# Cross attention and FP4 FFN on one core: x and h turned by DMA transposes instead of TensorE

## What is computed

```python
x = x + xattn(layernorm(x), ctx, ctx, Wt, Wp, Wg, Wz, gamma, beta)   # three 256x256 products, group statistics
x = x + ffn(layernorm(x))
# ffn: q() is blockwise FP4 (16 numbers a block), scale and grid, along the last dimension
gate = q(x) @ q(w_gate).T ; y = q(x) @ q(w_up).T                     # 1408 columns each
h = silu(gate) * y ; out = q(h) @ q(w_down).T                        # back to 512
```

## Time and profile before

| | us |
|---|---|
| median of 3 runs | 1983.17 (1981.67 to 1985.04) |
| the profiled execution, its own time | 1983.16 |
| its span, first to last instruction | 1981.2 |
| TensorE busy / VectorE busy in it | 1844.4 / 1610.4 |
| an odd tile and the even one behind it, mid loop | 28.36 + 27.57 |

### The profile page before, as it was taken

One profiled execution on the slowest core, in us unless ns is written; L12 is line 12 of the kernel. 1 busy time (PEld: TensorE's weight loads), 2 busy tenths in 40 slices (PEclk: granted clock), 3 DMA queues, 4 the chain that ended last, 5 costly groups with the idle time before them and its releaser, 6 DMA issues.

```text
span 1981.2 us, 32391 instructions
## 1 busy us (share of the span) xinstructions
PE 1844.4 (93%) x11022; PEld 1208.4 (61%) x11022; DVE 1610.4 (81%) x2885; ACT 620.4 (31%) x981; POOL 737.0 (37%) x1065
## 2 busy tenths in 40 slices
PE   2528899999999999999999999999999999999997
PEld 1427566666666666666666666666666666666664
DVE  5575888888888888888888888888888888888775
ACT  2324332333333332333233333333333333323221
POOL 4647443333333343433333343333333433333310
PEclk9769999999999999999999999999999999999999
DMA  5100010001000000000000000000010000100000
GB/s 183 51 0 22 17 33 16 32 32 32 16 32 32 32 25 23 32 32 32 16 32 32 32 21 26 32 32 32 16 32 32 32 16 32 32 32 27 11 11 17
DMA packets 32022, 60.11 MB, mean 30 GB/s; under 512 B 3072, under 2 KB 4352, under 8 KB 32000
## 3 DMA queue, kind: packets, MB, share of 16 engines
q1 hardware_dynamic: 32000, 59.81, 8.9%
HBM read 43.03 MB, written 16.78 MB: 30 GB/s over the span
## 4 chain that ended last, share of the span: by engine, by line
PE 41%; issue 20%; POOL 15%; DVE 12%; DMA 6%; ACT 4%; SPq 1%; DVEq 1%; POOLq 0%; ACTq 0%
PE pairs L449 19%; PE obank L461 12%; DMA c_in<-in_ctx 5%; POOL c_lo L1123 5%; PE pairs L413 5%; PE ubank L413 2%; ACT early L694 2%; DVE hT_parts L753 2%; ACT c_hi L610 2%; POOL q_lo L1129 1%; DVE ln_st L809 1%; DVE x L805 1%; DVE xT_lo L753 1%; POOL att L1151 1%; DVE early L906 1%
## 5 line engine op out<-in xcount | busy, mean ns | idle before, releaser
L461 PE MATMUL obank<-w_parts,hT_parts 128*128 128x512 f16 x2112 | 467.1, 380 | 0.0
L461 PEld LDWEIGHTS obank<-w_parts,hT_parts 128*128 128x128 f16 x2112 | 207.0, 98 | 235.4 <-issue 1.1
L449 PE MATMUL pairs<-w_gate_hi,xT_hi 128*128 128x352 f16 x1024 | 321.0, 313 | 7.8 <-DVE xT_lo L753 7.1
L449 PE MATMUL pairs<-w_gate_hi,xT_lo 128*128 128x352 f16 x1024 | 320.8, 313 | 0.0
L449 PE MATMUL pairs<-w_up_lo,xT_hi 128*128 128x352 f16 x1024 | 320.7, 313 | 0.0
L449 PE MATMUL pairs<-w_up_hi,xT_lo 128*128 128x352 f16 x1024 | 320.7, 313 | 0.0
L449 PE MATMUL pairs<-w_gate_lo,xT_hi 128*128 128x352 f16 x1024 | 320.7, 313 | 0.0
L449 PE MATMUL pairs<-w_up_hi,xT_hi 128*128 128x352 f16 x1024 | 320.5, 313 | 0.0
L897 DVE SCALAR_TENSOR_TENSOR h<-pairs,w_unit,early 128x352 f32<-128x352 f32 x256 | 149.5, 584 | 199.7 <-ACT early L694 195.6
L694 ACT ACTIVATE early<-pairs,w_unit 128x352 f32<-128x352 f32 x256 | 140.1, 547 | 366.3 <-PE pairs L449 366.3
L1123 POOL TENSOR_TENSOR c_lo<-c_in,c_hi 128x512 fp32r<-128x512 f32 x64 | 98.2, 1554 | 179.8 <-ACT c_hi L610 172.9
(11 more groups left out here) (172 smaller groups left out, 3615.7 us busy)
## 6 DMA issues: line engine op xcount, KB each, us to landing
x_in<-in_x SPq DMA_DIRECT2D x32, 512.0 KB, 3.4
c_in<-in_ctx SPq DMA_DIRECT2D x32, 512.0 KB, 3.5
out<-early SPq DMA_DIRECT2D x64, 256.0 KB, 2.1
raw<-in_L_ffn_w_down SPq DMA_DIRECT2D x2, 1408.0 KB, 8.8
raw<-in_L_ffn_w_gate SPq DMA_DIRECT2D x2, 1280.0 KB, 8.3
w_parts<-in_L_ffn_w_up SPq DMA_DIRECT2D x2, 1280.0 KB, 9.2
raw<-in_L_ffn_w_gate SPq DMA_DIRECT2D x2, 128.0 KB, 8.4
early<-in_L_xattn_Wt SPq DMA_DIRECT2D x1, 256.0 KB, 9.8
```

The costliest lines, as they stand in the source:

```text
L449: mm = pe.matmul(pairs[:, pair, n, 0:GW], xT[s][part][:, k, :], w1[n][wpart][:, k, c * GW:(c + 1) * GW], start=(k == 0 and part == 0 and w ...
L461: mm = pe.matmul(obank[:, :], hT[part][:, k, :], w2[wpart][:, k, :], start=(k == 0 and part == 0 and wpart == 0), stop=(k == KH - 1 and pa ...
```

## The change

x and h are no longer turned on TensorE. ScalarE casts hq (two pieces of 704 columns) and xq from SBUF to f16, VectorE subtracts, both also from SBUF, and both halves lie side by side in raw's second third (hq_parts, xq_parts). SyncE's queue then issues one DMA transpose for h (128 x 2816 numbers) and one for x (128 x 1024) in each tile, behind the load of the tile and ahead of the store. TensorE waits once for each. On ScalarE h's casts stand ahead of ctx_hi and the first Silu, x's ahead of the fourth Silu, and affine behind it. On VectorE h's subtractions stand behind h_finish, ahead of the first gated product; x's ahead of the residual. Blank and unchanged lines are left out of this diff, and some of its waits and of the start's lines:

```diff
--- before.py
+++ after.py
@@ -141,7 +141,8 @@
-        xT = [[sb(f"xT{s}_{part}", [P, KD, P], F16) for part in ("hi", "lo")] for s in range(2)]
+        xT_parts = [sb(f"xT_parts{s}", [P, 2, KD, P], F16) for s in range(2)]
+        xT = [[xT_parts[s][:, part] for part in range(2)] for s in range(2)]
@@ -157,6 +158,10 @@
+        hq_parts = raw[:, 1, 0:H].bitcast(F16).rearrange("p (a k) -> p a k", a=2)
+        xq_parts = raw[:, 1, H:H + D].bitcast(F16).rearrange("p (a k) -> p a k", a=2)
+        HPIECES = ((0, H // 2), (H // 2, H))
@@ -351,6 +356,20 @@
+            def turn_x(t, s):
+                made = t + 1 if isinstance(t, int) else sp.to_reg(t + 1)
+                wait_apart(sp, minus_made, x_lo_done, made)
+                sp.dma_start_transpose(xT_parts[s][:].rearrange("p a k n -> p (a k) n"),
+                                       xq_parts.rearrange("p a k -> p (a k)")).then_inc(x_turned, 16)
+            def turn_h(j):
+                made = 2 * j + 2 if isinstance(j, int) else sp.to_reg(2 * j + 2)
+                wait_apart(sp, minus_made, h_lo_done, made)
+                sp.dma_start_transpose(hT_parts[:].rearrange("p a k n -> p (a k) n"),
+                                       hq_parts.rearrange("p a k -> p (a k)")).then_inc(h_turned, 16)
@@ -372,9 +391,11 @@
+            turn_x(0, 0)
+                more = not isinstance(i, int) or i + 1 < NB
@@ -382,6 +403,10 @@
+                        turn_h(j - 1)
+                    if more or s == 0:
+                        turn_x(j + 1, 1 - s)
+                    if not isinstance(j, int) or j > 0:
@@ -389,6 +414,7 @@
+            turn_h(NT - 1)
@@ -425,21 +451,6 @@
-            def turn_x(t, bank):
-                pe.wait_ge(xq_ready, t + 1)
-                for k in range(KD):
-                    mm = pe.transpose(bank[:, k * P:(k + 1) * P], xq[:, k * P:(k + 1) * P], ident[:, :])
-                mm.then_inc(x_turned, 1)
-            def turn_h(j, r):
-                pe.wait_ge(hq_ready, 3 * j + r + 1)
-                k0, nk = SETS[r]
-                for k in range(nk):
-                    mm = pe.transpose(tbank[:, (r + 1) % 2, k, :], hq[:, (k0 + k) * P:(k0 + k + 1) * P], ident[:, :])
-                mm.then_inc(h_turned, 1)
@@ -454,12 +465,11 @@
-                for r, (k0, nk) in enumerate(SETS):
-                    pe.wait_ge(h_lo_done, 3 * j + r + 1)
-                    for k in range(k0, k0 + nk):
-                        for part, wpart in PARTS:
-                            mm = pe.matmul(obank[:, :], hT[part][:, k, :], w2[wpart][:, k, :],
-                                           start=(k == 0 and part == 0 and wpart == 0), stop=(k == KH - 1 and part == 1))
+                pe.wait_ge(h_turned, 16 * j + 16)
+                for k in range(KH):
+                    for part, wpart in PARTS:
+                        mm = pe.matmul(obank[:, :], hT[part][:, k, :], w2[wpart][:, k, :],
+                                       start=(k == 0 and part == 0 and wpart == 0), stop=(k == KH - 1 and part == 1))
...
@@ -538,7 +546,7 @@
-                    pe.wait_ge(x_lo_done, j + 1)
+                    pe.wait_ge(x_turned, 16 * j + 16)
@@ -551,32 +559,20 @@
-                        if c > 0 and not first:
-                            if c != 2:
-                                at_least(pe, h_lo_done, 3 * (j - 1) + (c - 2 if c == 3 else 0))
-                            turn_h(j - 1, c - 1)
+                        if isinstance(j, int) and j == 1:
+                            pe.wait_ge(w_lo_done, len(weight_sets))
-                    if more or s == 0:
-                        if first:
-                            pe.wait_ge(w_lo_done, len(weight_sets))
-                        at_least(pe, h_lo_done, 3 * (j - 1) + 2)
-                        turn_x(j + 1, tbank[:, 0].rearrange("p k n -> p (k n)"))
-            for r in range(3):
-                pe.wait_ge(h_lo_done, 3 * (NT - 1) + max(r - 1, 0))
-                turn_h(NT - 1, r)
@@ -603,6 +599,17 @@
+            def x_hi(t):
+                act.wait_ge(xq_ready, t + 1)
+                at_least(act, x_turned, 16 * t)
+                nc.scalar.copy(xq_parts[:, 0, :], xq[:, :]).then_inc(x_hi_done, 1)
+            def h_hi(j):
+                at_least(act, h_turned, 16 * j)
+                for r, (a, b) in enumerate(HPIECES):
+                    act.wait_ge(hq_ready, 2 * j + r + 1)
+                    nc.scalar.copy(hq_parts[:, 0, a:b], hq[:, a:b]).then_inc(h_hi_done, 1)
...
@@ -684,9 +690,13 @@
+                    if not first:
+                        h_hi(j - 1)
+                        if c == 3 and (more or s == 0):
+                            x_hi(j + 1)
@@ -698,15 +708,10 @@
-                        if c > 0 and not first:
-                            k0, nk = SETS[c - 1]
-                            split_hi(hT[0][:, k0:k0 + nk, :], c % 2, nk, h_turned, 3 * (j - 1) + c, h_hi_done)
-                        if c == 2 and more:
+                        if c == 3 and more:
-                    if more or s == 0:
-                        split_hi(xT[1 - s][0][:, :, :], 0, KD, x_turned, j + 2, x_hi_done)
...
@@ -839,7 +843,7 @@
-                at_least(dve, x_turned, t)
+                at_least(dve, x_hi_done, t)
@@ -882,10 +886,20 @@
-                for r, (k0, nk) in enumerate(SETS):
-                    at_least(dve, h_turned, 3 * (j - 1) + r + 1)
-                    a, b = k0 * P, (k0 + nk) * P
+                at_least(dve, h_hi_done, 2 * j)
+                for a, b in HPIECES:
+            def h_lo(j):
+                for r, (a, b) in enumerate(HPIECES):
+                    dve.wait_ge(h_hi_done, 2 * j + r + 1)
+                    nc.vector.tensor_tensor(hq_parts[:, 1, a:b], hq[:, a:b], hq_parts[:, 0, a:b],
+                                            ALU.subtract).then_inc(h_lo_done, 1)
+            def x_lo(t):
+                dve.wait_ge(x_hi_done, t + 1)
+                nc.vector.tensor_tensor(xq_parts[:, 1, :], xq[:, :], xq_parts[:, 0, :],
+                                        ALU.subtract).then_inc(x_lo_done, 1)
...
@@ -1025,14 +1036,11 @@
+                        h_lo(j - 1)
-                        if c > 0 and not first:
-                            k0, nk = SETS[c - 1]
-                            split_lo(hT[1][:, k0:k0 + nk, :], hT[0][:, k0:k0 + nk, :], c % 2, nk, h_hi_done,
-                                     3 * (j - 1) + c, h_lo_done)
@@ -1053,6 +1061,8 @@
+                    if quant_x:
+                        x_lo(j + 1)
@@ -1063,8 +1073,6 @@
-                    if quant_x:
-                        split_lo(xT[1 - s][1][:, :, :], xT[1 - s][0][:, :, :], 0, KD, x_hi_done, j + 2, x_lo_done)
@@ -1076,9 +1084,7 @@
-            for r, (k0, nk) in enumerate(SETS):
-                split_lo(hT[1][:, k0:k0 + nk, :], hT[0][:, k0:k0 + nk, :], (r + 1) % 2, nk, h_hi_done,
-                         3 * (NT - 1) + r + 1, h_lo_done)
+            h_lo(NT - 1)
```

More of the change, by code:

```diff
@@ L527, in _ @@
                     group_spread(t)
-                if n == 8:
-                    turn_x(0, obank)
             def body(i):
@@ L667, in _ @@
                 if n == 8:
-                    act.wait_ge(x_turned, 1)
-                    nc.scalar.copy(xT[0][0][:, :, :].rearrange("p k n -> p (k n)"), obank[:, :]).then_inc(x_hi_done, 1)
+                    x_hi(0)
                 if n == 5:
@@ L716, in _ @@
             grain(hm[:, :], h[:, :], h_y_done, NT, h_grain_done)
-            for r, (k0, nk) in enumerate(SETS):
-                split_hi(hT[0][:, k0:k0 + nk, :], (r + 1) % 2, nk, h_turned, 3 * (NT - 1) + r + 1, h_hi_done)
+            h_hi(NT - 1)
         @block.vector
@@ L895, in gated @@
                 if c == 0:
-                    at_least(dve, hq_ready, 3 * j)
+                    at_least(dve, hq_ready, 2 * j)
                 nc.vector.scalar_tensor_tensor(out=h[:, c * GW:(c + 1) * GW], in0=pairs[:, (s + 1 + c) % 2, 1, 0:GW],
@@ L972, in _ @@
                 if n == 9:
-                    dve.wait_ge(x_hi_done, 1)
-                    nc.vector.tensor_tensor(xT[0][1][:, :, :].rearrange("p k n -> p (k n)"), obank[:, :],
-                                            xT[0][0][:, :, :].rearrange("p k n -> p (k n)"),
-                                            ALU.subtract).then_inc(x_lo_done, 1)
+                    x_lo(0)
                 if n == 6:
```

## The result

The change makes the kernel slower: median 2012.09 us (4 runs, 2011.88 to 2013.69) against 1982.66, ratio 1.0148 [1.0131, 1.0166]. The forecast was 1967, faster. Two single runs of the experiments, 2012.89 in number 6 and 2642.36 in number 8, were slow ones with a mean granted clock of 0.932 and 0.656, and are in none of the figures. The profiled execution took 2011.88, its span is 2010.0, 28.8 more than before.

The account below looks back on a forecast made before the run. TensorE was taken to bound both tiles, with a second chain close behind in odd ones. Loop -16, start -3.9, last tiles -3, end +5.6 and +2, together -16 from 1983.16: forecast 1967 us, range 1946 to 2120.

Parts of the forecast that it names:

- The new order of VectorE's queue: Subtractions ahead of the first gated product put it at 11.8 us after the odd tile's scores start (S).
- the third group's: TensorE's idle time ahead of its third group, waiting for the first gated product: under 1 us.
- h turn: DMA transpose of h, 128 x 2816 f16, on SyncE's queue: taken as 6 us.
- cover: Time from the h turn's issue to the output product: 7.9 us in even tiles, 10.6 in odd ones.
- Rival 1: TensorE waits for a late h turn ahead of the output product: slower, about 2025 to 2420 us; chance 0.33.
- Rival 2: The chain behind the first gated product eats all the gain, 0.5 us more a pair: 1983 us; chance 0.12.
- The step that failed: Odd tile: spread at S+18.1, then 0.24 + 3.58 for the fourth group and 7.12 for output: 29.0 us.
- The pair: Odd tile 29.0 plus even tile 26.4: 55.4 instead of 55.93 us, -0.5 times 31 pairs, -16.
- the 6.27 between gated product and spread: Odd tile's normalise1, q_hi, q_lo and columns keep their distances: 6.27 us, nothing added for c_lo.
- The ends: Start -3.9 us; last two tiles -3; after the last to_q +5.6, and +2 (at most +8) for slower matmuls.
- Affine costed at zero: Affine behind the fourth Silu at the tile's end: zero by cover; without it up to 1 us a tile.

Follow-up runs that it names:

- number 6: Changed kernel with h's subtractions later in all tiles, plus copy_group and GpSimd's columns moved earlier: 1894.47 us; kernel before with only those two earlier moves: 1959.87 us.
- number 8: Affine put back behind the third Silu: in the changed kernel 2051.19 us; in the changed kernel as reordered in number 6, 1936.00 us.
- experiment 1: Changed kernel with 11 unread matmuls ahead of the group spread in odd tiles from tile 3 on: 1983.93 us, ratio 1.0012.
- experiment 2: Kernel before, TensorE's turns kept, with an unused GpSimd product ahead of columns in odd tiles: 2045.02 us, ratio 1.0321.
- experiment 3: Changed kernel with ScalarE's ctx_hi moved ahead of h's casts in odd tiles: 1995.93 us, ratio 1.007.
- experiment 9: Changed kernel with a second, unread DMA transpose of the same size ahead of h's own: 2045.48 us, ratio 1.0319.
- experiments 4 and 5: Changed kernel with h's casts behind the first Silu and its subtractions later: odd tiles only, 1947.79 us; all tiles, with ln1 behind copy_group, 1942.92 us.
- the fastest version: Changed kernel as reordered in number 6, with copy_group ahead of h's subtractions in odd tiles: 1880.26 us, ratio 0.9485.

## Why the prediction was wrong

**What held.** The new order of VectorE's queue: gated product at S+11.70 (S+11.8). The spread at S+18.57 (S+18.1), its wait 2.48 ("some 2 us"), the third group's 0.50 ("under 1"). Odd tile 29.33 (29.0), even 26.34 (26.4). h turn 5.2 us (6), x turn 3.1 (2.5), cover 8.1 and 11.2 (7.9 and 10.6). Rival 1, the late h turn, is false: no tile of the loop waits for it, and doubling it costs 0.57 an even tile. The 22 blocks land in 5.2 us, 0.24 each. The Trainium skill (VectorE: DVE Perf Modes, The three transpose paths) gives 1309 ns for one 128 x 128 block by DMA; taken per block in a row this would have been 28.8 (an estimate by that figure), and the runs contradict that use of the figure. Rival 2 was the closest to the mechanism, the chain behind the gated product, but it gave no change. That 2012 lies inside the wide range, 1946 to 2120, is luck: its upper part stood for late turns.

**The step that failed** is in the odd tile: "So the spread comes at 11.8 + 6.27 = S+18.1. After it 0.24 + 3.58 for the fourth group and 7.12 for the output: 29.0." The place and length of the wait were right, and the work behind it was priced at the full granted clock that the rows of before show. In those rows of the loop the longest wait was 0.48, so they could not tell what an idle time of 2.5 does. The prediction knew of it at the end, where "after that idle time its 33 matmuls may take more than 8.12: +2, at most +8", but put it at nothing in the loop and set no bound there, though the trace of before had such a fall behind its wait of 3.49 at 209.21. In 18 of 29 tiles the matmuls behind the wait run at half the clock for 3.41 us: +30 us, two thirds of the distance between −16 and +28.8. Filling the wait takes 28 of it away (experiment 1), a longer wait in the kernel before, without turns, brings falls (2), and with two shorter waits in its place there is none (3).

**The pair** (an odd and an even tile) was mis-sized: −0.24 without falls instead of −0.5, so 8 us over the loop. The term is the 6.27 between gated product and spread, which measured 6.87: c_lo "meets normalise1 instead, as its second half does now (1.33 for two), so nothing is added for that", but normalise1 took 1.95.

**The ends** are 6 us off. The last part came out at +5.4, forecast −3 + 7.6 = +4.6: to_q's end to the output 7.2 (7.9), the 33 matmuls 8.69 (8.12, +2 taken). The start gave −2.15 instead of −3.9, and tile 1, not costed, +3.4: a wait of 3.05 for the x turn and one of 4.02 for its first gated product. That was read off the trace and not tested.

**Affine costed at zero** has the wrong reason: "Nothing on TensorE waits for either until its first group of the next tile". VectorE waits, and its queue is the chain that reaches the next tile's first gated product, whose lateness the same text had worked out. The number itself held, as to_q starts at S+7.66 in the odd tile where 7.6 was forecast: with the x cast ahead of the Silu and affine behind it VectorE starts a tile as before, so this term has no visible part in the miss. Experiment 8 prices the move at 39 us in this kernel (0.6 a tile, within the text's up to 1 us a tile). This move is a good part of the change, and without it the kernel would be at 2051.

**A sum of rival 1.** By its own terms the pair at T = 10 is 28.4 + 29.0 = 57.4, not 57.1, and at T = 8.6 27.0 + 29.0; nothing above rests on it.

**Left open.** Why a wait of the same length is followed by a fall in some tiles and not in others, and why two waits of 1.8 and 1.5 in a tile are followed by none. How low the odd tile's last 0.4 us could go (26.43 against 26.09 of work). The start and the end weren't varied.

## What to carry to other kernels

When a change takes work off TensorE but delays the chain that feeds it, price the new wait twice: by its length, and by what the granted clock does behind it; look in the trace of the kernel before, its start included, for a wait of that length and what follows it. A few matmuls that nobody needs were worth 28 us here, and two shorter waits in place of a long one 16; the real cure is to move what the late chain doesn't need (here the subtractions, and q_lo ahead of columns) behind it. A queue that isn't waited for by the bounding engine in this tile may still set when the next tile's chain starts, so "nothing waits" has to be asked across the tile's end.

## What the runs showed of the hardware

- TensorE's granted clock fell to half for 3.41 us behind waits for the spread of 2.48 us in 18 of 29 odd tiles (kernel after) and 27 of 29 (experiment 9), of 1.9 to 2.0 in 11 of 29 (experiment 2), of 1.7 to 1.9 in 5 and 11 of 29 (experiments 4 and 5); never in experiment 3, with waits of 1.8 and 1.5 in one tile (29 tiles). In experiment 8 it fell for 6.83 in ten tiles.
- A DMA transpose of 128 x 2816 f16 within SBUF lands in 5.2 us and holds SyncE's queue for 3.3 to 3.4; one of 128 x 1024 in 3.1 and 1.23. The queue's packets rose from 32000 to 281856 and the DMA share of a tile from 0.09 only to 0.26 to 0.29. The 88 ns of a packet before is no price for a packet of a transpose: over the kernel after the mean is 25.8% x 16 x 2010 us / 281856 = 29 ns.
- Steps of VectorE and GpSimd get longer when they run at the same time: to_q takes 1.69 alone and 2.77 beside c_lo, the subtractions 1.69 and 2.75 beside c_lo (experiment 3), normalise1 0.99 alone (experiment 3), 1.33 beside a part of c_lo and 1.95 beside most of it, q_lo 2.49 and 2.98 beside the subtractions, c_lo 2.67 beside normalise1 and 3.34 beside to_q. A new order that removes one such meeting easily makes another: in the fastest version to_q is back at 1.70, and normalise1 takes 2.29.
